# The pooled tokens as a 65th selected token, and values and mix as one product

## The reference

```
normed = ln(x, g1, b1)                                    # 375 x 192
scores = sigmoid(normed @ Wr + br)                        # 375
idx    = the 56 tokens with the lowest scores
attn_out = softmax(q k^T / 4) v @ Wo + bo                 # 12 heads of 16, needed for those 56 only
w      = scores / (sum(scores) + 1e-6)
pooled = w @ normed                                       # 192
mix_out = (normed + scores[:, None] * pooled) @ Wm + bm
merged = attn_out where selected, else mix_out
h = x + merged;  out = h + gelu(ln(h) @ W1 + bf1) @ W2 + bf2
```

## Time and profile before

| | |
|---|---|
| median of 3 runs | 596.38 us (595.72 to 602.4) |
| the profiled execution | 596.45 us, span 594.7 us |
| PE busy | 519.1 us (87%) |
| DVE busy | 430.7 us (72%) |
| ACT busy | 237.0 us (40%) |
| POOL busy | 68.4 us (12%) |
| mean granted PE clock | 0.941 |
| share of the chain: PE, DVE, ACT, issue | 57%, 18%, 13%, 9% |

### The profile page before, as it was taken

The page is one execution under the profiler, slowest core; times in us unless marked ns, Lnnn a source line. Parts: engine busy times, 40 slices in busy tenths (PEclk is TensorE's granted clock), DMA queues, the critical chain, the costliest instruction groups (busy, mean ns, idle before and its releaser), DMA issues.

```text
span 594.7 us, 9326 instructions
## 1 busy us (share of the span) xinstructions
PE 519.1 (87%) x3248; PEld 421.8 (71%) x3248; DVE 430.7 (72%) x1247; ACT 237.0 (40%) x627; POOL 68.4 (12%) x67
## 2 busy tenths in 40 slices
PE   1637498969999999999999999999999999968896
PEld 1426376748876888688876987797778877856586
DVE  6787668586888888898788888888878483953240
ACT  1134113531457135812582257414660458114621
POOL 0010001101120003001210121011200130001000
PEclk9986599697999999999999999999999999978699
DMA  8431000010001000010001000100000000000001
GB/s 240 129 101 34 6 1 2 0 40 1 2 0 37 7 19 1 2 40 19 0 0 39 19 0 0 39 19 0 0 0 10 12 1 0 2 21 0 2 7 33
DMA packets 8281, 13.13 MB, mean 22 GB/s; under 512 B 1896, under 2 KB 6722, under 8 KB 8253
## 3 DMA queue, kind: packets, MB, share of 16 engines
q1 hardware_dynamic: 8253, 12.77, 7.7%
HBM read 10.46 MB, written 2.30 MB: 21 GB/s over the span
## 4 chain that ended last, share of the span: by engine, by line
PE 57%; DVE 18%; ACT 13%; issue 9%; POOL 1%; DMA 1%; DVEq 0%; ACTq 0%; SPq 0%; POOLq 0%
PE xb L1205 9%; PE zb L1109 7%; PE xb L1151 6%; ACT probs L988 3%; PE xb L1160 3%; ACT w_sq L913 3%; DVE w_sq L517 3%; ACT w_s L912 2%; DVE junk L525 2%; DVE dw L404 2%; PE xb L1186 2%; PE yb L1116 2%; PE yb L1381 2%; PE xb L1141 2%; PE xb L1142 2%
## 5 line engine op out<-in xcount | busy, mean ns | idle before, releaser
L826 POOL TENSOR_TENSOR rs<-ve,half 125x3 f32<-125x3 f32 (+1 forms) x32 | 33.5, 1046 | 399.5 <-DVE ve L369 323.7
L386 DVE SCALAR_TENSOR_TENSOR dw<-x_in,w_dw_sb,dw 96x750 f32<-96x750 f32 x84 | 79.0, 990 | 0.2
L1205 PE MATMUL xb<-scratch,w_sq 128*125 128x192 f32 x288 | 52.0, 343 | 4.4 <-ACT scratch L924 4.4
L1205 PEld LDWEIGHTS xb<-scratch,w_sq 128*125 128x125 f32 x288 | 50.6, 200 | 5.3 <-DVE scratch L539 5.3
L1381 PE MATMUL yb<-w_sb,gelu 128*125 128x192 f32 x252 | 48.1, 333 | 0.0
L1381 PEld LDWEIGHTS yb<-w_sb,gelu 128*125 128x125 f32 x252 | 40.7, 187 | 3.6 <-issue 2.8
L993 ACT ACTIVATE probsT<-zb 125x384 f32<-125x384 f32 x48 | 26.8, 559 | 20.2 <-PE zb L1316 20.2
L1151 PE MATMUL xb<-dft_n_sb,pooled_h 125*96 125x376 f32 x96 | 34.0, 506 | 1.0 <-DVE pooled_h L420 0.9
L924 ACT ACTIVATE scratch<-w_out_sb,natt 128x192 f32<-128x192 f32 x24 | 9.2, 445 | 63.4 <-DVE natt L537 63.4
L1316 PEld LDWEIGHTS zb<-ident_sb,probs 128*125 128x125 f32 x144 | 22.1, 203 | 15.6 <-issue 11.7
L1010 ACT ACTIVATE n2T<-zb 128x375 fp32r<-128x375 f32 (+1 forms) x16 | 7.7, 481 | 62.8 <-PE zb L1101 62.6
(11 more groups left out here) (208 smaller groups left out, 1284.3 us busy)
## 6 DMA issues: line engine op xcount, KB each, us to landing
x_in<-in_x SPq DMA_DIRECT2D x8, 567.0 KB, 4.3
out<-res_f SPq DMA_DIRECT2D x7, 281.2 KB
gelu<-in_w_qkv SPq DMA_DIRECT2D x1, 768.0 KB, 6.5
gelu<-in_w SPq DMA_DIRECT2D x1, 768.0 KB, 4.3
w_out_sb<-in_w_out SPq DMA_DIRECT2D x1, 576.0 KB
w_sb<-in_w SPq DMA_DIRECT2D x1, 576.0 KB
rows_sb<-in_rows SPq DMA_DIRECT2D x1, 504.0 KB
dft_n_sb<-in_dft_n SPq DMA_DIRECT2D x1, 493.5 KB
```

The lines of the kernel that those rows point to most:

```text
L386: ins = dve.scalar_tensor_tensor(out=dw[0:C, c, :], in0=src, scalar=w_dw[:, c, k:k + 1], in1=dw[0:C, c, :], op0=ALU.mult, op1=ALU.add)
L826: pool.tensor_tensor(out_[:], in_[:], half3[:] if len(in_.shape) == 3 else half3[:, 0, :], ALU.pow).then_inc(rs.sem, 1)
L1205: ins = mm(o, u[:, j, tok(t)], w_oa[:, j, :], start=(j == 0), stop=(j == IT - 1))
```

## The change

1. **One product for values and mix.** `w_v` and the split `w_m` become one tensor `w_vm` of 386 columns. `keys_values` writes each tile's 386 columns to a bank of its own (`zb[., t]`); the third waits for the first key copy. `mixed` is gone. DVE adds the mix part to `zed` (`block_mix`, two operations) ahead of `ranks`.
2. **The pooled tokens as a 65th slot.** `put` has a 65th column, the scores; `nr` is laid out in two halves of 97 columns, a column of ones in the first. `selected` so gathers the weighted sum of all tokens and the sum of scores as the 65th column of `nsT`, and `selected_mix` multiplies it with `w_m` as its 65th row. Three small DVE operations (`pooled_row`, now after `front_input`) divide and write row 65 of `att`. Row 65 of `putT` holds the scores of the tokens that weren't selected (`unselected_scores`, one DVE operation). `replaced` starts its own accumulation and adds everything.
3. **What goes**: on PE `pooled_sums`, `pooled_columns`, `pooled_row`, `mixed`; on DVE the old pooled operations, `score_row` and the low part of the pooled row; on ACT two copies of the pooled row.
4. **What moves**: PE: `forward_up(r, 2)` ahead of `ranks`; `selected_mix` behind `front_input` and `logits(q, 0)`. ACT: `selected_mix` behind `front_input`. DVE: the depthwise taps are (0,4), (4,5), (5,6), (6,7), none in every step, before it (0,3), (3,4), (4,5), (5,6), (6,7) in all but the first: the last pair of operations, ahead of `token_max`, goes to the first place, ahead of `scores`.
5. **New waits**: PE's `ranks` waits for `v_done` and `zm_done` (block_mix), `selected` for `sc_copied`, `turn(b, 1)` for `ms_done` and `pl_steps`; `logits(b, 0)` no longer waits for `ms_done`.

```diff
-        w_v = sb("w_v_sb", [C + 1, 2, CT, DV], fp32r)
+        w_vm = sb("w_vm_sb", [C + 1, 2, CT, DV + D], fp32r)
...
-        nr = sb("nr", [P, T, D + 2])
+        nr = sb("nr", [P, T, CT, C + 1])
...
             def scores(b):
...
-                dve.reciprocal(nr[:, :, D], sexp[:]).then_inc(sc_steps.sem, 1)
+                dve.reciprocal(nr[:, :, 1, C], sexp[:]).then_inc(sc_steps.sem, 1)
+                dve.reciprocal(put[:, :, Q], sexp[:]).then_inc(sc_steps.sem, 1)
+            def block_mix(b):
+                dve.wait_ge(*z_done.of(b))
+                for k, (t0, t1) in enumerate(((0, 2), (2, 3))):
+                    dve.wait_ge(*v_done.of(b, k + 1))
+                    dve.tensor_tensor(zed[:, t0:t1, :], zb[0:P, t0:t1, DV:DV + D], zed[:, t0:t1, :], ALU.add).then_inc(zm_done.sem, 1)
...
+            def unselected_scores(b):
+                dve.wait_ge(*sc_copied.of(b))
+                dve.scalar_tensor_tensor(out=putT[Q:Q + 1, 0:N], in0=zb[Q:Q + 1, 2, 0:N], scalar=SEL - 0.5, in1=score_row[Q:Q + 1, 0:N],
+                                         op0=ALU.is_gt, op1=ALU.mult).then_inc(sc_row_done.sem, 1)
+            def pooled_row(b):
+                dve.wait_ge(*ms_done.of(b))
+                dve.tensor_scalar(pl[Q:Q + 1, 0:1], zb[Q:Q + 1, 3, 256 + D:256 + D + 1], 1e-6, None, ALU.add).then_inc(pl_steps.sem, 1)
+                dve.wait_ge(*pl_steps.of(b, 1))
+                dve.reciprocal(pl[Q:Q + 1, 1:2], pl[Q:Q + 1, 0:1]).then_inc(pl_steps.sem, 1)
+                dve.wait_ge(*pl_steps.of(b, 2))
+                if not first(b):
+                    dve.wait_ge(*mix_ready.before(b))
+                dve.tensor_scalar(att[Q:Q + 1, :], zb[Q:Q + 1, 3, 256:256 + D], pl[Q:Q + 1, 1:2], None, ALU.mult).then_inc(pl_steps.sem, 1)
...
-                taps = ((0, 4), (4, 5), (5, 6), (6, 7), (7, 7), (7, 7)) if first(p) else ((0, 3), (3, 4), (4, 5), (5, 6), (6, 7), (7, 7))
+                taps = ((0, 4), (4, 5), (5, 6), (6, 7), (7, 7), (7, 7))
...
+                    block_mix(q)
                     ranks(q)
...
             def keys_values(b):
                 if not first(b):
                     act.wait_ge(*ql_ready.before(b))
                 for c in range(CT):
+                    act.wait_ge(*k_ready.of(b, c + 1))
+                    act.activation(kT[:, c, 0:N], zb[0:C, 2 + c, 0:N], ACT.Identity, bias=b_k[:, c:c + 1]).then_inc(kT_done.sem, 1)
                 for k, (t0, t1) in enumerate(((0, 2), (2, 3))):
                     act.wait_ge(*v_ready.of(b, k + 1))
                     if k == 0 and not first(b):
                         act.wait_ge(*pv_ready.before(b))
+                    act.activation(sexp[:, t0:t1], zb[0:P, t0:t1, D], ACT.Exp, scale=-1.0).then_inc(sexp_done.sem, 1)
                 for k, (t0, t1) in enumerate(((0, 2), (2, 3))):
+                    act.activation(v[:, t0:t1, :], zb[0:P, t0:t1, 0:D], ACT.Copy).then_inc(v_done.sem, 1)
...
+            def copy_scores(b):
                 act.wait_ge(*less_done.of(b))
+                if not first(b):
+                    act.wait_ge(*sc_row_done.before(b))
+                act.activation(score_row[Q:Q + 1, 0:N], zb[Q:Q + 1, 3, 0:N], ACT.Copy).then_inc(sc_copied.sem, 1)
...
-                    score_row(q)
+                    unselected_scores(q)
...
+                    dve.tensor_tensor(w_o[C:C + 1, 0, :], w_o[C:C + 1, 0, :], w_m32[C:C + 1, 0, :], ALU.subtract).then_inc(bias_done.sem, 1)
...
-                    score_row(q)
+                    copy_scores(q)
...
-                    pooled_row(q)
                     selected(q)
                 if last:
                     gelus(r, 4)
                     gelus(r, 5)
+                if front:
+                    front_input(p)
                 if middle:
                     selected_mix(q)
-                if front:
-                    front_input(p)
...
+                    ins.then_inc(k_ready.sem, 1)
+                for t in range(T):
+                    if t == 2:
+                        pe.wait_ge(*kT_done.of(b, 1))
+                    o = zb[0:P, t, 0:DV + D]
+                    split_product(o, nT[:, :, 0, tok(t)], w_vm[:, :, 0, :], True, False)
+                    ins = split_product(o, nT[0:C, :, 1, tok(t)], w_vm[0:C, :, 1, :], False, True)
...
             def ranks(b):
+                pe.wait_ge(*zm_done.of(b))
                 pe.wait_ge(*less_done.of(b))
                 for t in range(T):
-                    ins = mm(zb[0:Q, 3, 0:N], ones_bf[:], less[:, t, 0:N], start=(t == 0), stop=(t == T - 1))
+                    ins = mm(zb[0:Q + 1, 2, 0:N], ones_bf[:], less[:, t, 0:N], start=(t == 0), stop=(t == T - 1))
...
-                    cols = chan(0) if c == 0 else slice(C, D + 1)
+                    n = C + 1 - c
                     for t in range(T):
-                        ins = mm(zb[0:C + c, 3, Q * c:Q * c + Q], nr[:, t, cols], put[:, t, :], start=(t == 0), stop=(t == T - 1))
+                        ins = mm(zb[0:n, 3, (Q + 1) * c:(Q + 1) * c + Q + 1], nr[:, t, c, 0:n], put[:, t, :], start=(t == 0), stop=(t == T - 1))
...
+            def selected_mix(b):
+                mm(zb[0:Q + 1, 3, 256:256 + D + 1], nsT[:, 0, :], w_m[:, 0, :], start=True, stop=False)
+                mm(zb[0:Q + 1, 3, 256:256 + D + 1], nsT[0:C, 1, :], w_m[0:C, 1, :], start=False, stop=True).then_inc(ms_ready.sem, 1)
...
-                    pe.wait_ge(*ms_done.of(b))
...
+                if j == 1:
+                    pe.wait_ge(*ms_done.of(b))
+                    pe.wait_ge(*pl_steps.of(b))
...
-                ins = mm(zb[0:P, 2 + t // 2, D * (t % 2):D * (t % 2) + D], putT[:, tok(t)], att[:], start=False, stop=True)
+                ins = mm(zb[0:P, 2 + t // 2, D * (t % 2):D * (t % 2) + D], putT[:, tok(t)], att[:], start=True, stop=True)
...
                 if front:
                     over_channels(p)
-                if middle:
-                    pooled_sums(q)
+                if last:
+                    forward_up(r, 2)
+                if middle:
                     ranks(q)
                 if last:
-                    forward_up(r, 2)
                     forward_up(r, 3)
                 if middle:
                     slots(q)
-                    pooled_columns(q)
                 if last:
                     forward_up(r, 4)
                 if middle:
-                    pooled_row(q)
                     selected(q)
                 if last:
                     forward_up(r, 5)
                 if middle:
-                    selected_products(q)
+                    selected_queries(q)
                 if front:
                     front_input(p)
                 if middle:
                     logits(q, 0, r)
+                    selected_mix(q)
...
                 if middle:
                     context(q)
-                    mixed(q, 0)
                 if front:
                     spread(p, 4)
                 if middle:
-                    mixed(q, 2)
                     attention_out(q)
                 if front:
                     spread(p, 5)
...
                     forward_down(r, 2, 0)
                     forward_down(r, 2, 1)
                 if middle:
-                    replaced(q, 0)
-                    mixed(q, 1)
-                    replaced(q, 1)
-                    replaced(q, 2)
+                    for t in range(T):
+                        replaced(q, t)
```

More of the change, by code:

```diff
@@ L606, in ranks @@
                 for t in range(T):
-                    dve.scalar_tensor_tensor(out=less[:, t, tok(t)], in0=zb[0:P, 2, tok(t)], scalar=nr[:, t, D:D + 1], in1=later[:],
+                    dve.scalar_tensor_tensor(out=less[:, t, tok(t)], in0=zb[0:P, 3, tok(t)], scalar=nr[:, t, 1, C:C + 1], in1=later[:],
                                              op0=ALU.is_equal, op1=ALU.mult).then_inc(eq_done.sem, 1)
@@ L977, in selected_mix @@
                     act.wait_ge(*att_done.before(b))
-                act.activation(msel[:], zb[0:Q, 1, 0:D], ACT.Copy).then_inc(ms_done.sem, 1)
+                act.activation(msel[:], zb[0:Q, 3, 256:256 + D], ACT.Copy).then_inc(ms_done.sem, 1)
             def exponentials(b, j):
```

157 lines of the change are left out of this document (47 added, 110 removed).

## The result

The changed kernel takes 620.36 us (median of 4 runs, 616.71 to 621.45), the kernel before beside it 599.35 (595.72 to 602.40): a ratio of 1.0364, 95% interval 1.0306 to 1.0422. It is slower. The forecast was 606.0, its range 598 to 624, and slower by over 2% was the likeliest of the three outcomes with 0.49. So the range held, but the time is 14 us above the case that I had called the likeliest; what came is the mechanism of that case and the clock's rival on top of it.

The account below looks back on a forecast made before the run. It took a chain through PE up to `front_input`, then ACT and DVE until `token_out`, as the bound. A full step's +1.9 - 0.5 = +1.4 us, six times, plus the ends gave +9.6 on 596.38: 606.0 us, range 598 to 624.

Parts of the forecast that it names:

- the clock's rival: PE's new waits make its clock fall: 618 us if in three of six steps, 630 in all; chance 0.36.
- PE is the bound: Rival: PE's busy share is what counts, so a batch saves 3.4 us of PE, giving 569 us; chance 0.05.
- Values and mix in one product: On PE, 18 matmuls widen from 194 to 386 columns: +1.2 us, upper bound +1.7; the score exponential comes later by it.
- Comparisons +1.5: On DVE, the comparisons wait for `block_mix` and start at about 288.45 instead of 286.95 us.
- `ranks` +2.95: On PE, `ranks` queues behind `forward_up(2)`, which waits 1.8 us for the first gelu; `ranks` starts 2.95 us later.
- `front_input` +1.2: On PE, `front_input` moves from 299.64 to 300.85 us because `even` ends later on DVE.
- exponential +1.9: On ACT, `msel` waits for PE's moved mix and delays the table load; the first exponential comes 1.9 us later.
- `token_out` -0.5: With `mixed` gone from PE, `token_out` starts when the scaled weights are there, 0.5 us a step gained.
- The table load: On ACT, ahead of the exponential: trace load 1.28 us, exponential 1.64 after its start, preferred to the skill's 2.66 us switch.
- Six steps +8.4: The six full steps, with three batches in flight, each take 1.4 us more, +8.4 together.
- Step 1 +1.3, step 8 -0.4: Step 1 lacks the forward part, +1.3 us; step 8 lacks the front, loses 1.3 and gains 1.7 from *mixed*, -0.4.
- Absorbed delays: Rival: unseen ACT or DVE slack between `front_input` and `token_out` lets only half of the 1.4 arrive, 601 us; chance 0.12.

Follow-up runs that it names:

- e_all_order: Changed kernel with `ranks` ahead of `forward_up(2)`, gelus 0 and 1 ahead of the score copy, `selected_mix`, `msel` and `pooled_row` ahead of `front_input`: 598.67 us, ratio 1.000.
- e_ranks_first: Changed kernel with one pair exchanged on PE, `ranks` ahead of `forward_up(2)` as in the kernel before: 606.65 us, ratio 1.013.
- e_before_fill: Kernel before plus useless PE products in its first two steps and the step without a front part: 587.73 us, ratio 0.982.
- e_best_fill: Changed kernel, mended orders, block's mix a separate product behind `ranks`, useless PE products in first two steps and step without front part: 579.65 us, ratio 0.968.

## Why the prediction was right and where it was wrong

- **What bounds the kernel.** Right: PE lost 10 us of work and the time rose. The rival "PE is the bound" (569) is out.
- **Values and mix in one product**, +1.2. Right in size: 3.34 us, 3.18 from its start to that of the next product, against 1.95; 0.177 a matmul where I took 0.175.
- **Comparisons +1.5, `ranks` +2.95, `putT` +2.15, norm +1.5, `front_input` +1.2, exponential +1.9, `token_out` -0.5.** Each but the last came within 0.15 us (the table above), whichever start of `token_out` before is taken; the -0.5 is -0.47 by the chain and -0.30 by the timeline. The experiments turn two of these steps around: undoing the place of `ranks` gives 0.78, undoing the place of the mix 0.81, together what the change had cost. I had priced both, but not seen that together they are the whole loss; that the new product with all that it replaces comes out even once the orders are mended (62.69 against 62.77) follows from my own sum, 1.2 less 0.7 of pooled operations on DVE less 0.5 at `token_out`, and I didn't draw it.
- **The table load.** The first exponential comes 1.43 us after the load's start (1.64 in the earlier trace rows), with no drain ahead of the load. The Trainium skill's (ScalarE: Activation LUTs, What ACT_TABLE_LOAD costs) 2.66 us for a switch isn't what this place shows; the sum by the trace was right.
- **Six steps +8.4.** The steps measured +9.0 (64.27 against 62.77, six times). Right.
- **Step 1 +1.3, step 8 -0.4.** Wrong. Step 1 is 2.7 longer, the last part 4.7. With the clock held up in both kernels the last part is 72.8 against 71.6 us, +1.2 where I had -0.4; the other 3.5 are clock. The gain of 1.7 that I counted from *mixed* doesn't show. In step 1 the granted clock is 0.80 against 0.86; no run parts what the waits cost there from what the clock does.
- **The clock.** This is the step that failed: the sum has no term for it. I gave it 0.36 and put it beside the forecast, though the forecast itself had PE wait 1.8 and 1.3 us at two places, and the earlier trace rows showed a fall behind two of three stretches with such waits. It fell in five of six full steps. Its price was wrong the other way: I took 4 us a fall, for 9 us of PE work at half clock; measured are 1.4, with the granted clock at 0.50 for only 3.4 us in three of the five falls and 6.8 in two. And I looked for it in the full steps alone: of the 23.8 us between the two spans some 9.0 are the waits of the full steps, 7.1 are clock in them, and of the 7.4 in step 1 and the last part 3.5 are shown to be clock. Count and price erred in opposite ways: five falls at my 4 us would have given 626, beyond the range. So it is luck in part that 620 lies within it, and slower by over 2% came true only with the clock; the waits alone are about 9 us, 1.5%. The Trainium skill (TensorE: Matmul & The Clock Gate, Why this matters for your kernels) warns only of longer idle gaps; falls inside or within 0.9 us behind gaps of 1.41 to 1.56 us, as in the changed kernel, contradict it as a guide here.
- **Absorbed delays** (601). Out: a delay ahead of the first exponential arrives at `token_out` whole, but for the 0.5.

What stays open is which pattern of waits lets the clock fall, and so how often a new order will make it fall; the falls were counted in one execution of each kernel. The undisturbed step of the changed kernel has the same two waits as those that fell; e_all_order falls with waits of 0.85 and 0.67 us, e_ranks_first with its 1.15 doesn't. No run here tells what decides it.

## What to carry to other kernels

Costing a moved instruction means asking who stands behind it in its queue: here two changes of place cost 0.8 us a step each, together the whole loss at full clock; with both undone the rest of the change, the wider product with it, comes out even (62.69 us against 62.77). When PE isn't the bound, taking work off it can cost time: here its new idle time let the clock fall, and the products behind it on the chain paid; read the clock in the prologue and the epilogue too, not only in the loop. A few useless matmuls in a wait of PE are a cheap test for this, and here the cheapest gain as well.

## What the runs showed of the hardware

- 39 products of 128x128x128 in fp32, placed in PE's waits of one step, raised the granted clock of the last part from 0.76 to 0.96 and cut it from 82.9 to 72.8 us.
- A fall of the clock in a full step of the changed kernel cost 1.2 to 2.0 us, 1.4 on the mean of five; two in e_all_order cost 0.8 and 0.7.
- The kernel before scatters less with its ends covered: 587.15 to 588.94 us over six runs of e_before_fill, 595.79 to 602.66 over the eleven of the kernel before beside it. It isn't so for each: the six of e_best_fill go from 578.56 to 583.17.
